# Carry stationary and W moving in 512 columns: a two-way row scan with the product turned by 32x32 blocks

## The reference

```
step(carry, x):  new = relu(Wm @ carry + b) + x      # Wm is 1024 x 1024, carry is 1024 x (4*48)
down:  xs = rows of gn(x); carry = xs[0]; ys over xs[1:]
up:    carry = down[-1];  over down[:-1] in reverse, adding down[h]
result = x + stack of the up scan
```

## Time and profile before

| | |
|---|---|
| median of 3 runs | 1852.66 us (1851.65 to 1884.84) |
| profiled execution, its span | 1849.8 us |
| PE busy | 1717.1 us, 93%, 12,036 matmuls |
| DVE busy | 1197.4 us, 65%, 3282 instructions |
| ACT busy | 316.9 us, 17%, 763 |
| POOL busy | 646.1 us, 35%, 1145 |
| first matmul of the scan starts | 126.55 us |
| last matmul starts | 1845.56 us |
| DMA | 206 MB, 111 GB/s over the span |

### The profile page before, as it was taken

One profiled execution on the slowest core, in us unless ns is written; L12 is line 12 of the kernel. 1 busy time (PEld: TensorE's weight loads), 2 busy tenths in 40 slices (PEclk: granted clock), 3 DMA queues, 4 the chain that ended last, 5 costly groups with the idle time before them and its releaser, 6 DMA issues.

```text
span 1849.8 us, 33139 instructions
## 1 busy us (share of the span) xinstructions
PE 1717.1 (93%) x12036; PEld 1716.1 (93%) x12036; DVE 1197.4 (65%) x3282; ACT 316.9 (17%) x763; POOL 646.1 (35%) x1145
## 2 busy tenths in 40 slices
PE   0029999999999999999999999999999999999999
PEld 0029999999999999999999999999999999999999
DVE  7998666666666666666665666556565656566564
ACT  0011111111111111111111111111111111111111
POOL 0046444445444444444432222222222222222222
PEclk9999999999999999999999999999999999999999
DMA  9953222121212222220002242424333333424111
GB/s 352 368 188 120 95 76 102 68 103 68 102 68 103 76 94 87 83 97 23 0 0 78 110 153 102 153 102 154 115 140 124 132 134 122 147 108 153 51 51 51
DMA packets 61436, 206.07 MB, mean 111 GB/s; under 512 B 4160, under 2 KB 33856, under 8 KB 61376
## 3 DMA queue, kind: packets, MB, share of 16 engines
q1 hardware_dynamic: 61232, 205.54, 30.9%
q10 hardware_dynamic: 144, 0.00, 0.0%
HBM read 136.32 MB, written 69.21 MB: 111 GB/s over the span
## 4 chain that ended last, share of the span: by engine, by line
PE 91%; DMA 4%; DVE 4%; SPq 1%; issue 0%; ACT 0%; POOLq 0%; POOL 0%; DVEq 0%
PE bank L411 63%; PE bank L413 28%; DMA x_ring<-x_rows 2%; DMA d_ring<-x_rows 2%; DVE work L286 1%; SPq L142 1%; DVE d_ring L342 1%; DVE moments L297 0%; DVE carry L332 0%; DVE carry L334 0%; DVE w_lo L349 0%; DVE d_ring L365 0%; DVE summed L360 0%; DVE spread L311 0%; ACT work L273 0%
## 5 line engine op out<-in xcount | busy, mean ns | idle before, releaser
L411 PE MATMUL bank<-carry,w_hi 128*128 128x384 f32 x6016 | 1715.6, 360 | 13.2 <-DVE carry L334 10.0
L413 PE MATMUL bank<-carry,w_lo 128*128 128x192 f32 x6016 | 1507.6, 251 | 0.0
L413 PEld LDWEIGHTS bank<-carry,w_lo 128*128 128x128 f32 x6016 | 1151.2, 191 | 0.0
L411 PEld LDWEIGHTS bank<-carry,w_hi 128*128 128x128 f32 x6016 | 1131.1, 188 | 13.9 <-issue 9.9
L360 DVE TENSOR_TENSOR summed<-bank,work 128x192 f32<-128x192 f32 x752 | 267.0, 355 | 552.6 <-ACT work L273 531.9
L273 ACT ACTIVATE work<-bank,bias_sb 128x192 f32<-128x192 f32 x752 | 307.4, 421 | 1416.2 <-PE bank L413 1416.2
L243 POOL TENSOR_TENSOR x_ring<-x_ring,d_ring 128x192 f32<-128x192 f32 x384 | 228.8, 596 | 662.6 <-DVE carry L334 649.9
L334 DVE TENSOR_TENSOR carry<-d_ring,carry 128x192 fp32r<-128x192 f32 x752 | 337.7, 449 | 26.2
L223 POOL TENSOR_TENSOR xn<-x_ring,gn_mean 128x192 f32<-128x192 f32 x376 | 214.9, 572 | 396.2 <-DVE d_ring L365 387.1
L332 DVE CAST carry<-d_ring 128x192 fp32r<-128x192 f32 x752 | 197.2, 262 | 26.1
L226 POOL TENSOR_TENSOR xn<-xn,gn_rstd 128x192 f32<-128x192 f32 x376 | 191.5, 509 | 29.5
(11 more groups left out here) (24 smaller groups left out, 12.2 us busy)
## 6 DMA issues: line engine op xcount, KB each, us to landing
x_ring<-x_rows SPq DMA_DIRECT2D x88, 768.0 KB, 6.9
out_rows<-x_ring SPq DMA_DIRECT2D x47, 768.0 KB, 3.9
down_rows<-d_ring SPq DMA_DIRECT2D x40, 768.0 KB, 3.6
d_ring<-down_rows SPq DMA_DIRECT2D x40, 768.0 KB, 5.7
d_ring<-x_rows SPq DMA_DIRECT2D x12, 1536.0 KB, 16.2
x_ring<-x_rows SPq DMA_DIRECT2D x8, 1536.0 KB, 16.4
d_ring<-w_t SPq DMA_DIRECT2D x7, 512.0 KB, 8.9
out_rows<-x_ring SPq DMA_DIRECT2D x8, 96.0 KB, 1.6
```

The source lines that it names most:

```text
L411: pe.matmul(bank[m][:, 0:2 * COLS], w_hi[:, k, out_cols], carry[:, parity, k, :, :].rearrange("p s c -> p (s c)"), start=(k == 0), stop=False)
L413: last = pe.matmul(bank[m][:, 0:COLS], w_lo[:, k, out_cols], carry[:, parity, k, 0, :], start=False, stop=(k == K - 1))
```

## The change

The operands of the product change places. A row of 192 columns (4 images x 48) is cut into three **chunks** of 64 columns (4 images x 16). A chunk's scan needs only itself, so the three are independent **chains**; `i` counts chain steps in the order chunk 0, 1, 2 of row 1, chunk 0, 1, 2 of row 2, and so on: 282 of them (STEPS).

The carry is now the stationary operand, 128 columns of it: 64 of chain step j-1 and 64 of chain step j. W is the moving operand, 512 output channels at a time. **Job j** (283 of them) does, for eight input tiles k, three matmuls of 512 columns (hi*hi, hi*lo of W, lo*hi), 24 in all, for output half j % 2. So each chain step is in two jobs that follow each other, one per output half; the first half of its result is there after job i, the second after job i+1, and it is needed by job i+3. Job j waits for hi and lo of chain step j-3 before its first matmul and of j-2's first half before its fifth input tile (`wait_split`). Banks rotate over eight jobs.

The product comes out with carry columns on partitions and channels along the free axis, and must be turned:

1. DVE, `turn_blocks(j)`: one transpose of all 32x32 blocks of the first two quarters of the bank, 128 x 256, to `blocks` in SBUF; then for the other two quarters eight transposes of 32 x 128 (one for each pair of source and target quadrant) straight from PSUM to their place in `channels`.
2. ACT, `move_blocks(j)`: eight copies of 32 x 128 that bring `blocks` to the right partitions.
3. ACT, `rectify(j)`: four Relu with bias over 128 x 128, in place, after both.
4. DVE, `make_half(j, i)`: for each of the two chain steps, product + addend, 128 x 256, into d_ring.
5. ACT, `split_hi`, and POOL, `split_lo`: the two parts of the carry, 128 x 256 each, for each of the two.

POOL also normalises one chunk (two passes of 128 x 512) in each job of the down scan and adds one (128 x 512) in each job of the up scan. DVE's order is turn_blocks(j), wait for rectified(j), make_half twice, turn_blocks(j+1); ACT's is move_blocks(j), rectify(j), split_hi twice, move_blocks(j+1). The rows of d_ring are now laid out by tile, chunk, image, column. W comes in 16 loads of 256 KB and is split in 16 tiles of 512 columns (13 lo parts on POOL, three on DVE); row 0 is normalised and split in four pieces by DVE and ACT. All engines' streams are written out without loops.

```diff
-        carry = sb("carry", [P, 2, K, 2, COLS], F32R)
+        st_hi = sb("st_hi", [P, K, 2 * P], F32R)
+        st_lo = sb("st_lo", [P, K, 2 * P], F32R)
...
+SLOT_AT = ((0, 0), (0, 1), (P, 1), (P, 0))
+PAIR_AT = ((0, 2), (0, 1), (1, 2), (P, 1))
+def blocks_of(j):
+    return ((j + 1) % 2, j % 2)
+def first_done(i):
+    return 2 * i + 1
+def second_done(i):
+    return 2 * i + 2
+def members(j):
+    return [i for i in (j - 1, j) if 0 <= i < STEPS]
...
+        def stationary(st, j, k):
+            if len(members(j)) == 1:
+                return slot(st, members(j)[0], k, k + 1).rearrange("p k c -> p (k c)")
+            base, step = PAIR_AT[j % 4]
+            return st[:, k, base:base + P] if step == 1 else st[:, k, base:base + 2 * P - base:2]
+        def source(t, q, u):
+            return t[q * B32:(q + 1) * B32, u * P:(u + 1) * P].rearrange("p (k a) -> p k a", k=KB)
+        def target(j, q, u):
+            return channels[j % 2][u * B32:(u + 1) * B32, :, q * B32:(q + 1) * B32]
...
         @block.gpsimd
+            def normalise(i):
...
+                pool.tensor_tensor(dst, x_chunk(h, c), table(gn_mean), ALU.subtract).then_inc(centred, 1)
+                pool.wait_ge(centred, i + 1)
+                pool.tensor_tensor(dst, dst, table(gn_rstd), ALU.mult).then_inc(xn_ready, 1)
...
+            for j in range(JOBS):
+                for i in members(j):
+                    if i < STEPS - CHUNKS:
+                        split_lo(j, i)
+                if j + XN_AHEAD < DOWN:
+                    normalise(j + XN_AHEAD)
+                if DOWN - CHUNKS <= j - 1:
+                    output(j - 1)
...
         @block.scalar
+            def move_blocks(j):
+                act.wait_ge(blocks_ready, j + 1)
+                for u in range(ACT_QUADS):
+                    for q in range(used(j) // B32):
+                        final = act.activation(target(j, q, u), source(blocks, q, u), ACT.Copy)
+                final.then_inc(blocks_moved, 1)
+            def rectify(j):
+                act.wait_ge(blocks_moved, j + 1)
+                act.wait_ge(direct_done, j + 1)
+                for kk in range(KB):
+                    k = (j % 2) * KB + kk
+                    cols = channels[j % 2][:, kk, 0:used(j)]
+                    final = act.activation(cols, cols, ACT.Relu, bias=bias_sb[:, k:k + 1])
+                final.then_inc(rectified, 1)
...
         @block.vector
+            def turn_blocks(j):
+                dve.wait_ge(acc_ready, j + 1)
+                dve.transpose(blocks[0:used(j), :], bank[j % BANKS][0:used(j), 0:ACT_QUADS * P]).then_inc(blocks_ready, 1)
+                if j >= 2:
+                    dve.wait_ge(y_ready, first_done(j - 2))
+                for u in range(ACT_QUADS, QUADS):
+                    for q in range(used(j) // B32):
+                        final = dve.transpose(target(j, q, u), source(bank[j % BANKS], q, u))
+                final.then_inc(direct_done, 1)
...
+                dve.tensor_tensor(here, product_of(j, i), addend, ALU.add).then_inc(y_ready, 1)
...
         @block.tensor
+            for j in range(JOBS):
+                o = j % 2
+                out = bank[j % BANKS][0:used(j), :]
+                if j >= BANKS:
+                    pe.wait_ge(direct_done, j - BANKS + 1)
+                for n in range(K):
+                    k = KB * blocks_of(j)[n // KB] + n % KB
+                    final = n == K - 1
+                    wait_split(hi_ready, first_hi, j, n)
...
+                    pe.matmul(out, stationary(st_hi, j, k), w_cols(w_hi, o, k), start=(n == 0), stop=False)
...
+                    pe.matmul(out, stationary(st_hi, j, k), w_cols(w_lo, o, k), start=False, stop=False)
+                    wait_split(lo_ready, first_lo, j, n)
+                    last = pe.matmul(out, stationary(st_lo, j, k), w_cols(w_hi, o, k), start=False, stop=final)
+                    if final:
+                        last.then_inc(acc_ready, 1)
```

More of the change, by code:

```diff
@@ L26, with row_of @@
 P = 128
-SLOTS = 8
+K = 8
+KB = 4
+C = 1024
+H = 48
+NI = 4
+WIDTH = 48
+COLS = NI * WIDTH
+CHUNKS = 3
+W16 = WIDTH // CHUNKS
+Q = 64
+HALF = 512
+B32 = 32
+QUADS = 4
 GN_GROUP = 32
 GN_EPS = 1e-5
+BN_DIM = 6
+RING = 8
+GROUPS = H // RING
+LAST = GROUPS - 1
 STAT_CHUNKS = 4
-DVE_LO = 3
-WAVE = 5
-BN_DIM = 6
-def build(nc, x_rows, w_t, bias, down_rows, out_rows):
[L37 to L48, removed]
+TC = K // STAT_CHUNKS
+ROWS = H - 1
+STEPS = CHUNKS * ROWS * 2
+DOWN = CHUNKS * ROWS
+JOBS = STEPS + 1
+XN_SLOTS = 4
+ACT_QUADS = 2
+BANKS = 8
+W_TILES = 16
+W_POOL = 13
+XN_AHEAD = 2
+SLOT_AT = ((0, 0), (0, 1), (P, 1), (P, 0))
+PAIR_AT = ((0, 2), (0, 1), (1, 2), (P, 1))
+def row_of(i):
+    step = i // CHUNKS
+    return step + 1 if step < ROWS else 2 * ROWS - 1 - step
+def blocks_of(j):
[6 more added lines that the diff above has]
+    return [i for i in (j - 1, j) if 0 <= i < STEPS]
+def build(nc, x_rows, w_t, bias, down_rows, out_rows):
     with ExitStack() as ctx:
@@ L165, in _ @@
[L165 to L200, removed]
@@ L228, in _ @@
[L228 to L243, removed]
-                                       ALU.add).then_inc(out_ready, 1)
@@ L255, in _ @@
+            for i in range(XN_AHEAD):
+                normalise(i)
+            for j in range(JOBS):
[6 more added lines that the diff above has]
+                    output(j - 1)
         @block.scalar
@@ L268, in _ @@
[L268 to L274 removed]
+            act.activation(gn_std[:, :], bank[7][:, 0:K * NI], ACT.Sqrt, bias=eps[:, 0:1]).then_inc(std_ready, 1)
+            for t in range(3, K):
+                w_round(t)
@@ L276, in _ @@
+            for j in range(JOBS):
+                move_blocks(j)
+                rectify(j)
+                for i in members(j):
+                    if i < STEPS - CHUNKS:
+                        split_hi(j, i)
         @block.vector
@@ L397, in _ @@
+            for j in range(JOBS):
+                turn_blocks(j)
+                dve.wait_ge(rectified, j + 1)
+                for i in members(j):
+                    make_half(j, i)
         @block.tensor
```

394 lines of the change are left out of this document (204 added, 190 removed).

## The result

The changed kernel takes **1700.8 us** (1700.6 to 1700.9, four runs); its ratio to the kernel before is **0.918**, interval [0.917, 0.920]. So it is faster by 8%. The forecast was 1633 with a range of 1590 to 1730. The direction and the range held; the case I called likeliest did not come. TensorE sets the time, not the cycle of VectorE and ScalarE. That the range held is partly luck: for the case that came it was 1590 to 1612, and 1700.8 lies inside only because the range was made wide for another case, a longer cycle. The runs of before fall in two levels, near 1852 and near 1885 us; the ratio compares the first with the runs of after.

A forecast was written before the change was run, and what follows sets the result against it. TensorE, busy 93%, was taken to bound the kernel, its 192-column matmuls held by weight loads. After the change: start 141 + 282 x 5.26 (VectorE and ScalarE cycle) + end 5.8 = 1630, plus 2.9 for the runs' median: 1633 us, range 1590 to 1730.

The forecast's parts named there:

- the case I called likeliest: The serial cycle of VectorE and ScalarE sets the time, 5.2 to 5.45 us a job: 1615 to 1690 us; 46%.
- a longer cycle: VectorE and ScalarE's cycle takes 5.45 to 6.1 us, small transposes spaced 0.40: 1690 to 1870 us; 16%.
- Columns as before, little over half the matmuls, loads covered: TensorE: columns 3.48 million against 3.47, matmuls from 12,032 to 6,792, each 213 ns covering a load of 107 to 124.
- The theory that the 192-column matmul lasted as long as a weight load: Kernel before: the 192-column matmul is bound by a weight load, 107 to 124 ns; the 384-column one is not.
- the change doesn't do what it says: Columns, not loads, set TensorE's rate at 0.493 ns each: 6.06 us a job, 1851 us; 4%.
- TensorE at 216 ns a matmul, 5.18 us a job: Price of a 512-column matmul after the change, between bounds of 213.3 and 252 ns; 24 of them a job.
- The cycle, forecast at 5.23 by the sum and 5.26 with jitter: VectorE and ScalarE's serial chain per job (transposes, Relus, make_half, handovers), just above TensorE's 5.18 us; bounds 4.3 and 5.75.
- PE sets, 25%: TensorE sets the time because the transposes overlap: 150 + 279 x 5.18 + 9.1 + 2.9 = 1607 us, 1590 to 1612.
- The 131 ns matmul: Sustained 512-column matmuls with loads at 131 ns, 3.1 us a job; with overlapping transposes 1376 us, 1%.
- GpSimd late in the down scan: GpSimd's 16-element runs at double price need 7.7 us a job and delay make_half: 344 us more, 1977; 8%.
- The coupling: A VectorE operation with two SBUF inputs waits out GpSimd's running one; cost 0 in the loop, one turn each at the start.
- Start and end: First matmul at 124.5 us after five VectorE turns behind GpSimd, first cycle ending at 141; end 5.8 after the last cycle.

The follow-up runs named there:

- runs 5 and 6: Kernel before, second matmul of each pair 128 columns wide for 192 (run 5: 1865.6 us) or 256 wide (run 6: 1904.3 us); kernel before on the same chip 1851.5.
- run 6: Kernel before with the second matmul of each pair 256 columns wide for 192: 1904.3 us, beside 1851.5 for the kernel before on the same chip.
- run 1: Changed kernel with carry slots in a ring of six, every sixth chain step written twice, so no stationary has stride 2: 1678.1 us.
- run 7: Changed kernel without w_lo times carry hi for five of eight input tiles a job, 19 matmuls for 24: 1638.6 us.
- run 10: Kernel of run 1, with GpSimd waiting before its fourth W tile until VectorE has normalised row 0's first chunk: 1676.9 us.
- run 4: Kernel of run 1, with the third product of seven of eight input tiles written to another bank and left out: 1678.1 us.
- run 3: Changed kernel, some third-product matmuls replaced by bf16 ones of zeros (down scan) or cut to 128 columns (up scan): 1687.4 us.
- run 2: Changed kernel, third product cut to 384 columns for two of eight input tiles (down scan) or 256 for one (up scan): 1673.9 us.

## Why the prediction was right or wrong

**Columns as before, little over half the matmuls, loads covered: right.** The theory that the 192-column matmul lasted as long as a weight load is shown by runs 5 and 6. The case "the change doesn't do what it says" (columns at 0.493 ns, 1851 us) is refuted by the same runs.

**TensorE at 216 ns a matmul, 5.18 us a job: this is the step that failed.** It takes 230.0 and 5.52. I took 213.3 plus the 2 ns by which the pair at the lower clock exceeded its sum. That was a misreading: rows 5 show one pair, rounded to 0.54 us, and the kernel before takes 3.20 us for the six pairs from 127.17 to 130.37, 0.533 each, which is 640 / 1.2 GHz with no excess at all.

```profile
127.17 0.58 PE L411 MATMUL bank<-carry,w_hi 128*128 128x384 f32 x1
...
130.37 0.57 PE L411 MATMUL bank<-carry,w_hi 128*128 128x384 f32 x1
```

In the changed kernel's job 0, behind a wait of 6.85 us, the matmuls start every 0.427 us, 512 / 1.2 GHz exactly (the level is read from this spacing; the clock column of the profile says 1.00 there). So the excess can't be read at the lower level. At 2.4 GHz it is 13.3 ns, and 20 where the stationary has stride 2. The rows at the full clock had it: I put a pair between 160 + 107 = 267 and the measured 284, gave the whole difference to the load, and none to the 384-column matmul; with run 6's 13.3 it is 173 + 111. The stride I named, and priced at 0 on the ground that a load could double and still hide; it does hide, and costs 7 ns (run 1). The term is off by 283 x 24 x 14 ns = 95 us.

**The cycle, forecast at 5.23 by the sum and 5.26 with jitter: right in size (5.27 to 5.29), and not what sets the time.** Small transposes 314 ns in a spacing of 0.33, for 0.34 taken; the block transpose 450, for 410; two make_half 0.76 for 0.78; four Relus 1.29 for 1.15. The errors nearly cancel. The small transposes don't overlap one another: eight in 2.61 us are 0.33 from start to start, longer than one lasts. By the Trainium skill (VectorE: DVE Perf Modes, Two Vector instructions with no wait between them) an instruction whose start quadrant differs from the last one's waits for all before it; the trace agrees: none of the eight starts before the one ahead has ended, while the two make_half, which both start at partition 0, overlap (0.76 us for twice 0.42). ScalarE's moves, 8 in 2.57, tie with them, as the upper bound had it.

**"PE sets, 25%" is the case that came**, with its price wrong for the same reason. In its own formula 230 for 216 gives 150 + 279 x 5.52 + 9.1 + 2.9 = 1702; measured 1700.8. The transposes did not overlap, which I had made the condition of this case: it came for another reason, TensorE being slower than I had it.

**The 131 ns matmul** of the Trainium skill (TensorE: Matmul & The Clock Gate, Back-to-back issue gap) is not seen: in no run does a 512-column matmul cost less than 226.5 ns on average over a window.

**GpSimd late in the down scan (8%, 1977 us): did not come.** Passes with runs of 16 elements take 1.07 us for 1.21 forecast, the split 0.75 for 0.65, and the job is as long in both scans, even in run 7, where any wait of make_half would show. **The coupling** with VectorE is real and lies where the prediction put it, at the start (run 10).

**Start and end.** The first matmul came at 121.50 for 124.5: TensorE's first matmul needed two of VectorE's turns behind GpSimd, not five (it then waited 0.63 us for `st_lo`). The first cycle ended at 140.6 for 141, and the end took 8.9 us for 9.1. A late first cycle costs next to nothing when TensorE sets: TensorE waits 0.6 us before job 3 and not again, since the cycle is 0.25 us a job quicker and catches up.

## What to carry to other kernels

Read what a matmul costs from its start-to-start spacing, once in a stretch that its columns bound and once in one that the loads bound, and at the clock at which the kernel will run: a residue of a few per cent that one can assign to either side is worth 95 us over 6792 matmuls. Take such a spacing over many instructions: one pair read to 0.01 us gave an excess that wasn't there. When work leaves the engine that sets the time, add up the serial cycle of the engines that must keep pace, each instruction at its spacing, before trusting busy shares: 69% and 76% busy left a margin of 4%, and moving a quarter of the transposition either way made the kernel slower than before. Operands read with a stride can cost time even where the load is hidden; try the contiguous layout even if it means writing some of them twice.

## What the runs showed of the hardware

- A column-bound 128x512 matmul with its weight load costs 226.5 ns at the full clock: 213.3 + 13.3. The 13.3 ns don't depend on the bank written last (run 4), and no saving is seen with bf16, which next to fp32r settles little (run 3); the same constant fits 384 + 256 columns (run 6), while run 2's narrower matmuls among 512-column ones leave 2 to 8 ns more than it and the stride explain. At the lower clock it is not there (0.427 us for 512 columns, 0.533 for a pair). What it comes from stays open: in every run here each matmul has its own weight load, so a matmul without one was not tried.
- A matmul of 128 columns saves nothing over one of 192 or 256 (286.6, 284.3 and 293.2 ns a pair with a 384-column one).
- A stationary of 128 fp32r columns read with stride 2 adds 7 ns to a hidden load's matmul. Job 282, with 64 of them, does not show it: its matmuls start 0.227 apart.
- 32x32 block transposes on VectorE from PSUM: 450 ns for 128x256 and 314 for 32x128, with no overlap between neighbours that change quadrant; ScalarE's copies of 32x128 between quadrants behave alike (311 ns, spacing 0.32), while its four Relus of 128x128 (393 each, in 1.29 us) overlap by 0.1.
- VectorE's small operations with two SBUF inputs wait until GpSimd's running tensor_tensor has ended: 1.19 for 0.19 us, 1.42 for 0.42.
